# Causal attention in a two-layer tower: values as stationary weights in four column groups, exponentials head by head with bias and summed output

## What is computed

```python
def _L1_attn_ref(hidden_states, c_attn_w, c_attn_b, c_proj_w, c_proj_b):
    qkv = hidden_states @ c_attn_w + c_attn_b
    q, k, v = jnp.split(qkv, 3, axis=-1)
    q, k, v = (split_heads(q), split_heads(k), split_heads(v))      # 12 heads of 16
    scores = jnp.einsum('bhqd,bhkd->bhqk', q, k) / np.sqrt(hd)
    scores = jnp.where(causal[None, None, :, :], scores, mask_value)
    attn = jax.nn.softmax(scores, axis=-1)
    out = jnp.einsum('bhqk,bhkd->bhqd', attn, v)
    out = out.transpose(0, 2, 1, 3).reshape(B, S, D)
    return out @ c_proj_w + c_proj_b
```

## Time and profile before

| | us |
|---|---|
| median of 3 runs | 1743.46 (1740.56 to 1755.52) |
| the profiled execution, its own time | 1757.27 |
| span of the profiled execution | 1755.6 |
| PE, DVE, ACT, POOL busy | 1325.4, 819.8, 495.5, 494.0 |

### The profile page before, as it was taken

The page is one execution under the profiler, slowest core; times in us unless marked ns, Lnnn a source line. Parts: engine busy times, 40 slices in busy tenths (PEclk is TensorE's granted clock), DMA queues, the critical chain, the costliest instruction groups (busy, mean ns, idle before and its releaser), DMA issues.

```text
span 1755.6 us, 23414 instructions
## 1 busy us (share of the span) xinstructions
PE 1325.4 (75%) x7336; PEld 911.9 (52%) x7336; DVE 819.8 (47%) x1551; ACT 495.5 (28%) x834; POOL 494.0 (28%) x394
## 2 busy tenths in 40 slices
PE   0666687788768673988894678998998879999960
PEld 0212132332322362888884464665657469999950
DVE  2488975876688853111111635345463412222212
ACT  0445346446535210233231212415151101101100
POOL 4756644544544451000003400000000600000025
PEclk9868678889878875799997658898888889999985
DMA  4200000000000014888883100000000368888843
GB/s 118 43 1 0 1 1 1 1 1 1 1 1 1 1 55 144 240 256 250 241 263 89 48 1 0 1 0 0 0 1 3 108 178 242 245 242 239 245 129 94
DMA packets 56062, 152.96 MB, mean 87 GB/s; under 512 B 9632, under 2 KB 30880, under 8 KB 51200
## 3 DMA queue, kind: packets, MB, share of 16 engines
q1 hardware_dynamic: 44096, 127.80, 26.1%
q0 software_dynamic: 11904, 24.40, 4.6%
HBM read 133.09 MB, written 19.07 MB: 87 GB/s over the span
## 4 chain that ended last, share of the span: by engine, by line
PE 48%; DVE 16%; DMA 12%; issue 9%; POOL 5%; ACT 3%; DVEq 3%; POOLq 2%; SPq 1%; ACTq 1%; PEldq 0%
PE ps L720 35%; DMA expert<-arena 8%; DVE arena L1432 5%; PE ps L848 3%; PE ps L1090 3%; POOL arena L484 2%; DMA arena<-sorted 2%; DVE ps L1427 2%; PE ps L873 1%; PE ps L1082 1%; PE ps L986 1%; DVEq L1428 1%; ACT arena L587 1%; DVE st L1188 1%; POOL h_rows L350 1%
## 5 line engine op out<-in xcount | busy, mean ns | idle before, releaser
L720 PE MATMUL ps<-arena 96*128 96x128 f32 (+1 forms) x1680 | 224.1, 290 | 8.3 <-issue 8.3
L1432 DVE TENSOR_TENSOR_SCAN arena<-arena,ps 128x1024 f32<-128x1024 f32 x96 | 219.5, 2287 | 13.4
L720 PEld LDWEIGHTS ps<-arena 96*128 96x128 f32 (+1 forms) x1680 | 215.2, 192 | 12.4 <-issue 12.1
L720 PE MATMUL ps<-xTF,wreg 96*128 96x512 f32 x352 | 203.4, 725 | 9.0 <-DVE arena L1593 4.8
L848 PE MATMUL ps<-arena,pick 32*128 32x512 f32 x384 | 133.4, 778 | 95.9 <-DVE arena L1432 92.9
L472 POOL DMA_DIRECT2D expert<-arena x88 | 47.9, 544 | 508.5 <-DVE arena L1555 225.7
L385 POOL DMA_INDIRECT sorted<-x_rows,row_i x64 | 62.6, 979 | 414.1 <-DVEq L1337 395.3
L587 ACT ACTIVATE arena<-ps,wreg 128x508 f32<-128x508 f32 x192 | 120.9, 681 | 200.4 <-PE ps L860 199.6
L720 PE MATMUL ps<-arena,ew_in 96*128 96x128 f32 x1248 | 154.6, 284 | 7.7 <-issue 7.7
L720 PE MATMUL ps<-xT,wreg 96*128 96x512 f32 (+3 forms) x296 | 133.9, 599 | 29.7 <-ACT arena L548 15.6
L720 PEld LDWEIGHTS ps<-arena,ew_in 96*128 96x128 f32 x1248 | 150.2, 199 | 11.5 <-issue 11.4
(11 more groups left out here) (203 smaller groups left out, 1799.8 us busy)
## 6 DMA issues: line engine op xcount, KB each, us to landing
ew_in<-in_e_in SPq DMA_DIRECT2D x24, 768.0 KB, 6.3
arena<-in_e_in SPq DMA_DIRECT2D x24, 768.0 KB, 6.8
ew_out<-in_e_out SPq DMA_DIRECT2D x20, 675.0 KB, 5.5
arena<-in_e_out SPq DMA_DIRECT2D x20, 675.0 KB, 5.4
ew_in<-in_e_in SPq DMA_DIRECT2D x20, 576.0 KB, 5.1
arena<-in_e_in SPq DMA_DIRECT2D x20, 576.0 KB, 5.0
ew_out<-in_e_out SPq DMA_DIRECT2D x24, 384.0 KB, 6.6
arena<-in_e_out SPq DMA_DIRECT2D x24, 384.0 KB, 7.2
```

The costliest lines, as they stand in the source:

```text
L720: last = pe.matmul(o, lhs, rhs, start=(n == 0), stop=(n == len(pairs) - 1))
L1432: ve.tensor_tensor_scan(hid[k % 3], dec[k % 3], bx.rearrange("p x t -> p (x t)"), 0.0, ALU.mult, ALU.add)\
```

## The change

The softmax is taken apart differently. `masked(t)` no longer subtracts the maximum from all scores; it makes a small tensor `low`, the maximum times minus a quarter, 12 columns. ACT then does 12 exponentials per sequence, one per head (128x128), each with its column of `low` as bias and with the sum of its results going to a column of `den`. DVE gets a new step, `shared_out(t)`, which takes the reciprocal of the 12 sums and multiplies all 128x1536 probabilities by them, before they are turned.

The values now are the stationary operand: `vr` has 32 columns per head, 16 of them zero, and the 12 matmuls of `values(t)` write to four column groups (PSUM partitions 32b to 32b + 31) in three slots of 128 columns, with the turned probabilities streaming. The output therefore comes out transposed; DVE's `take_values(t)` copies it into `oT`, and the eight transposes and the copy to `xT` before the projection go. The projection weights are laid out to fit, three groups of 128 rows instead of two of 96, and lie in the tile `pick`, whose earlier contents are no longer used by then.

The order changes in two places. On ACT the exponentials of sequence t + 1 stand before the silu and the copies of sequence t. On DVE `shared_out(t - 1)` stands behind `masked(t)`.

```diff
-        vr = part(9216, CT * H * (HD + 1)).rearrange("p (t h d) -> p t h d", t=CT, h=H)
+        vr = part(9216, CT * H * 32).rearrange("p (t h d) -> p t h d", t=CT, h=H)
...
+        oT = part(22016, 3 * CN).rearrange("p (a t) -> p a t", a=3)
...
+        low = [part(16928 + 16 * k, H) for k in range(2)]
+        den = [part(16960 + 16 * k, H) for k in range(2)]
...
+                def weights(t):
+                    act.wait_ge(t_sm, i * CT + t + 1)
+                    for b in range(4):
+                        for a in range(3):
+                            h = 3 * b + a
+                            act.activation(sm[t % 2][:, b, a, :], sm[t % 2][:, b, a, :], ACT.Exp, bias=low[t % 2][:, h:h + 1],
+                                           scale=HD ** -0.5, accum_out=den[t % 2][:, h:h + 1])
+                    act.drain().then_inc(t_p, 1)
+
+                weights(0)
                 for t in range(CT):
-                    act.wait_ge(t_sm, i * CT + t + 1)
-                    act.activation(sm[t % 2], sm[t % 2], ACT.Exp, scale=HD ** -0.5)
-                    act.drain().then_inc(t_p, 1)
+                    if t + 1 < CT:
+                        weights(t + 1)
                     if not first:
                         shared_silu(i - 1, 3 + t, mixed_banks)
...
-                    for h in range(H):
-                        last = pe.matmul(ps[:, 1, h * (HD + 1):(h + 1) * (HD + 1)], pT[t % 2][:, h, :], vr[:, t, h, :],
-                                         start=True, stop=True)
+                    for a in range(3):
+                        for b in range(4):
+                            last = pe.matmul(ps[32 * b:32 * b + 32, 1, a * P:(a + 1) * P], vr[:, t, 4 * a + b, :], pT[t % 2][:, 4 * a + b, :],
+                                             start=True, stop=True)
...
-                        pe.wait_ge(t_p, i * CT + t + 1)
+                        pe.wait_ge(t_pn, i * CT + t + 1)
...
                 pe.wait_ge(t_or, i * CT + CT)
-                transposes(nr, 2).then_inc(t_oT, 1)
...
-                    last = accumulate(row_slot(4, j), [(xT[:, k, j * P:(j + 1) * P], wproj[:, k, :]) for k in range(2)])
+                    last = accumulate(row_slot(4, j), [(oT[:, a, j * P:(j + 1) * P], wproj[:, a, :]) for a in range(3)])
...
-                    ve.tensor_tensor(sm[t % 2], sm[t % 2], smax.rearrange("p (b a k) -> p b a k", b=4, k=1)
-                                     .broadcast_to((P, 4, 3, P)), ALU.subtract)
+                    ve.tensor_scalar(low[t % 2], smax, -HD ** -0.5, None, ALU.mult)
                     ve.drain().then_inc(t_sm, 1)
...
+                def shared_out(t):
+
+                    ve.wait_ge(t_p, i * CT + t + 1)
+                    ve.reciprocal(rden, den[t % 2])
+                    ve.drain()
+                    ve.tensor_tensor(sm[t % 2], sm[t % 2], rden.rearrange("p (b a k) -> p b a k", b=4, k=1).broadcast_to((P, 4, 3, P)), ALU.mult)
+                    ve.drain().then_inc(t_pn, 1)
+
+                def take_values(t):
                     ve.wait_ge(t_o, i * CT + t + 1)
...
+                    ve.tensor_copy(oT[:, :, t * P:(t + 1) * P], ps[:, 1, 0:3 * P].rearrange("p (a q) -> p a q", a=3))
                     ve.drain().then_inc(t_or, 1)
 
                 for t in range(CT + 2):
                     if t < CT:
                         masked(t)
+                    if 1 <= t <= CT:
+                        shared_out(t - 1)
                     if not first and 1 <= t <= CT:
                         shared_mul(i - 1, 2 + t, mixed_banks)
                     if t >= 2:
-                        over_sums(t - 2)
-                ve.wait_ge(t_oT, i + 1)
-                ve.tensor_copy(xT[:, :, :], ps[0:KH, 2:4, :])
-                ve.drain().then_inc(t_oTs, 1)
+                        take_values(t - 2)
```

More of the change, by code:

```diff
@@ L98, in tower @@
             (KH, 2, FF0 * P), (P, FF0, D), (KH, 2, D), (P, DG, P), (P, DG * NST)])
-        wqk, wv, wproj, ws1, ws3, ws2 = carve([
-            (KH, 2, 6 * P), (KH, 2, D), (KH, 2, D), (KH, 2, SF * P), (KH, 2, SF * P), (P, SF, D)])
+        wproj = pick[:, 0:3 * D].rearrange("p (a d) -> p a d", a=3)
+        wqk, wv, ws1, ws3, ws2 = carve([
+            (KH, 2, 6 * P), (KH, 2, D), (KH, 2, SF * P), (KH, 2, SF * P), (P, SF, D)])
         wr2 = sb("wr2", [KH, 2, E0])
@@ L143, in tower @@
         qkT = part(6144, 6 * CN).rearrange("p (f t) -> p f t", f=6)
-        vr = part(9216, CT * H * (HD + 1)).rearrange("p (t h d) -> p t h d", t=CT, h=H)
-        sm = [part(n, H * P).rearrange("p (b a k) -> p b a k", b=4, a=3) for n in (10240, 13824)]
-        pT = [part(n, H * P).rearrange("p (h q) -> p h q", h=H) for n in (11776, 15360)]
+        vr = part(9216, CT * H * 32).rearrange("p (t h d) -> p t h d", t=CT, h=H)
+        sm = [part(n, H * P).rearrange("p (b a k) -> p b a k", b=4, a=3) for n in (10752, 12288)]
+        pT = [part(n, H * P).rearrange("p (h q) -> p h q", h=H) for n in (13824, 15360)]
+        oT = part(22016, 3 * CN).rearrange("p (a t) -> p a t", a=3)
         xTS = xTF
-        rden = part(13312, H)
-        smax = part(13328, H)
+        smax, rden = part(16896, H), part(16912, H)
+        low = [part(16928 + 16 * k, H) for k in range(2)]
+        den = [part(16960 + 16 * k, H) for k in range(2)]
         actT1 = part(17920, SF * CN).rearrange("p (f t) -> p f t", f=SF)
@@ L218, in tower @@
         t_s, t_ms, t_sm, t_p, t_pt, t_pT, t_o, t_or = [sem(n) for n in ("t_s", "t_ms", "t_sm", "t_p", "t_pt", "t_pT", "t_o", "t_or")]
-        t_oT, t_oTs, t_pr, t_fn, t_fnT, t_fT = [sem(n) for n in ("t_oT", "t_oTs", "t_pr", "t_fn", "t_fnT", "t_fT")]
+        t_pn, t_pr, t_fn, t_fnT, t_fT = [sem(n) for n in ("t_pn", "t_pr", "t_fn", "t_fnT", "t_fT")]
         t_rs, t_rsr, t_g, t_u, t_sl, t_act, t_dn, t_ch = [sem(n) for n in ("t_rs", "t_rsr", "t_g", "t_u", "t_sl", "t_act", "t_dn", "t_ch")]
@@ L1117, in attention_chunk @@
                     shared_up(i - 1, 7, mixed_banks)
-                pe.wait_ge(t_oTs, i + 1)
                 for j in range(CT):
-                    last = accumulate(row_slot(4, j), [(xT[:, k, j * P:(j + 1) * P], wproj[:, k, :]) for k in range(2)])
+                    last = accumulate(row_slot(4, j), [(oT[:, a, j * P:(j + 1) * P], wproj[:, a, :]) for a in range(3)])
                 last.then_inc(t_pr, 1)
@@ L1579, in _ @@
             causal = cst[:, C_CAUSAL:C_CAUSAL + P].rearrange("p (a b k) -> p a b k", a=1, b=1).broadcast_to((P, 4, 3, P))
-            ve.memset(vr[:, :, :, HD:HD + 1], 1.0)
+            ve.memset(vr[:, :, :, HD:32], 0.0)
             def joined(i):
@@ L1632, in masked @@
                     ve.drain()
-                    ve.tensor_tensor(sm[t % 2], sm[t % 2], smax.rearrange("p (b a k) -> p b a k", b=4, k=1)
-                                     .broadcast_to((P, 4, 3, P)), ALU.subtract)
+                    ve.tensor_scalar(low[t % 2], smax, -HD ** -0.5, None, ALU.mult)
                     ve.drain().then_inc(t_sm, 1)
-                def over_sums(t):
-                    ve.wait_ge(t_o, i * CT + t + 1)
[L1640 to L1644, removed]
+                def shared_out(t):
[5 more added lines that the diff above has]
+                def take_values(t):
+                    ve.wait_ge(t_o, i * CT + t + 1)
+                    ve.tensor_copy(oT[:, :, t * P:(t + 1) * P], ps[:, 1, 0:3 * P].rearrange("p (a q) -> p a q", a=3))
                     ve.drain().then_inc(t_or, 1)
@@ L1765 @@
         w_qk=halves(np.concatenate([strips(wa[:, :D]), strips(wa[:, D:2 * D])], 1)), w_v=halves(wa[:, 2 * D:]),
-        w_proj=halves(a["L1_attn_c_proj_w"]), w_g=halves(a["L1_ffn_gate_w"].T),
+        w_proj=groups(strips(a["L1_attn_c_proj_w"].T).T), w_g=halves(a["L1_ffn_gate_w"].T),
         w_s1=halves(a["L1_ffn_sw1"].T), w_s3=halves(a["L1_ffn_sw3"].T), w_s2=groups(a["L1_ffn_sw2"].T),
```

## The result

The changed kernel takes 1806.4 us (median of four runs: 1796.6, 1804.9, 1807.8 and 3297.1), the kernel before, run beside it, 1749.5 (1740.6 to 1766.0). The run of 3297.1 stands apart and is left out of the ratio. The ratio is 1.030, 95% interval 1.018 to 1.041: slower. The profiled execution took 1807.84 us, its span 1806.2.

What follows compares the result with a forecast made beforehand. The prediction saw a latency chain passing between engines in four chunk stretches. Chunks 1 to 3 gain 22 us each (+66), chunk 0 gains 14, together +80 on 1743.5, giving 1823 us, range 1778 to 1866.

Steps and rivals of the forecast that it cites:

- What bounds it: In the four chunk stretches, a latency chain passing from engine to engine, none full; 81 us forecast for chunks 1 to 3.
- The small terms: In the chunk chain: mask step 3.9 us, division 2.15, output copy 0.55, values 0.95 to 1.66, projection 4.1.
- the heavier rival: In the chunks: exponential sets of 7.0 us (1853), lower clock throughout (1859), or column groups not overlapping (1855 to 1870); chance 0.10.
- E: ACT's set of 12 exponentials with sums per sequence: 5.1 us, the middle of 3.2 and 7.0; 16 sets add 58 us.
- The sums are nearly free: Rival on ACT's exponentials: a set takes only 3.2 us, 30 us less in all, total 1793; chance 0.16.
- PE's clock, the mis-sized term: PE's work in the chain of chunks 1 to 3: 25.2 us at the upper clock, 47 at the lower.
- I take the middle, 36: PE's share of the chain per chunk 1 to 3, set at 36 us between its upper and lower clock levels.
- Faster, the swap alone: Rival in the chunks: only the values swap counts, exponentials and division fit under PE's waits; -33 us, 1710; chance 0.05.
- Its deciding point: PE's wait before the first transposes of t = 1 and 2: ups still 9.8 us apart would show the faster case.
- PE keeps its upper clock: Rival in the chunks: shorter values and longer continuous pieces hold the clock; 70 us per chunk, total 1782; chance 0.06.

Runs made afterwards that it cites:

- the last edit: Kernel before with swapped values, old exponential, sums in the free rows, division through two block transposes, PSUM bank released after DVE's first transpose: 1722.1 us, ratio 0.983.
- silu first: Changed kernel with ACT's old order, silu and copies of a sequence ahead of the next sequence's exponentials, complete softmax: 1789.7 us.

## Why the prediction was right, and which terms were off

The forecast was 1823 (1778 to 1866); the result is 1806.4, slower as said. The mechanism was right, and two terms of the sum were too large; both erred to the same side, so nothing cancelled. By its steps:

**What bounds it.** Right. The forecast's chain, link by link in its order, is the chain of the profile after: scores(0), masked(0), two sets of exponentials, silu 3, up 3, third group, scores(2), masked(2), and so on to the last gate, up and projection. The waits for DVE's division and for the silu are there. Ups "some 15 us apart" were 17.2 and 18.3 for the first three, then 10.0; chunks of "75 to 90 us" were 72.5 to 75.1.

**The small terms.** Masked(t) 3.9: 3.93 measured (1205.46 to 1209.39). Shared_out 2.15: 2.11 and its hand-over. Take 0.55: 0.56. Values between 0.95 and 1.66: in chunk 2 they are 1.44, 1.35, 0.84 and 0.90; the column groups overlap, and the heavier rival's part on that falls. Gate 7, up 7 and projection 8.1: 7.77.

**E.** Taken as 5.1 between 3.2 and 7.0, measured 4.73. The floor was too low as well: without sums the heads are 0.294 us apart (3.62 less the first 0.386, over 11), not the 0.26 that six activations of the expert stage had given. "The sums are nearly free" falls: they cost 1.11 a set. Its total of 1793 lies no farther from the result than the forecast's 1823, but not for its reason, since E was not 3.2. With 16 sets on the chains the term was 6 us too large.

**PE's clock, the mis-sized term.** The step "I take the middle, 36" of PE per chunk, 37 with scores(0), was too high: in the chain of chunk 2 PE has 33.3 us, and 41.8 stand outside it against the 44.1 forecast (45.1 without scores(0)'s 0.95); of these 2.3, four sets make 1.5. In this chain the first three ups take 3.78 us each and the last one 1.72, and gate 7, up 7 and the projection are at the upper level too; there the waits before are short. Chunk 0 came to 57.6 instead of 63 for the same reason: PE 19.0 instead of 22, the rest 38.6 instead of 41. The mean of chunks 1 to 3 is 73.7 instead of 81. In sum the stretches grew by 52.8 instead of 80.

**Faster, the swap alone.** The forecast gave it -33. Measured -40.7, with neither sums nor division, and -34.2 in the last edit, with the whole softmax: the mechanism is real. The sum had no term for PE's clock, which went to 0.86 to 0.90. The Trainium skill's advice in "TensorEngine Tiling (Array Packing)", "Performance Considerations", is borne out here by the -40.7: the swap is the good part of this change. Its deciding point was named rightly: the ups followed each other at 17 us, not 9.8, so the case did not come about.

**"PE keeps its upper clock".** This fell: the granted clock is 0.59 in chunk 0 and 0.73 to 0.74 in the others.

## What to carry to other kernels

When three engines pass work in a ring, a microsecond added on ACT or DVE can cost one and a half: PE waits, and its next matmuls ran at the lower level here (heads: 28 us by length, 38 to 44 measured). It need not: with silu first, the division cost almost nothing in three of four chunks. Price the halves of a change apart: here the swap gained 41 us of stretch time, and exponentials per head, sums, division and their order lost 94. And look for the free rows first: the padding of the swapped values can carry the sums, and a bank can be given back when it has been read rather than when the result is done.

## What was not expected of the hardware

The summed output of an activation is a second instruction, 187 ns, of which 92 ns stay visible behind its neighbours (0.386 against 0.294 us a head). DVE's reciprocal takes (2556 - 229) / (384 - 12) = 6.3 ns per column between the two sizes, while a copy of 384 columns takes 557 ns in all; a turn of 32x32 blocks costs as much as a copy, 0.58 us, from PSUM too. And an added wait can leave the time as it was: 2.1 us of division in every step of chunks 1 to 3 lengthened these three chunks by 1.5 us in all (212.07 against 210.55), while PE's busy time in them fell by 23.7. What decides when PE's clock rises and falls was not tried.
